# A gather ring on one Trainium2 core: semaphores by section, or by octet of eight tiles

## What is computed

```python
msgs = features[edge_src] * edge_weight[:, None]
agg = jax.ops.segment_sum(msgs, edge_dst, num_segments=N_NODES, indices_are_sorted=True)
return jnp.einsum('ni,oi->no', agg, W) + b
...
H = jax.nn.gelu(xf @ W1 + b1, approximate=False)
probs = jax.nn.softmax((H @ Wg + bg) / TEMP, axis=-1)
assign = jnp.argmax(probs, axis=-1)
for e in range(Wd.shape[0]):
    y = H @ Wd[e] + bd[e]
    out = out + jnp.where((assign == e)[:, None], probs[:, e:e + 1] * y, 0.0)
...
x = x + _L0_gnn_ref(_layernorm(x, axis=-1), src, dst, edge_weight, L0_gnn_W, L0_gnn_b)
x = x + _L0_ffn_ref(_layernorm(x, axis=-1)[None], ...)[0]
```

## Time and profile before

| | us |
|---|---|
| median of three runs | 4119.44 |
| the three runs | 4086.34, 4121.28, 4119.44 |
| the profiled execution | 4089.45 |
| its span, first to last instruction | 4087.7 |
| busy: PE / PE weight load | 2198.2 (54%) / 1562.5 (38%) |
| busy: POOL / DVE / ACT | 1722.3 (42%) / 1026.6 (25%) / 625.3 (15%) |

### The profile page before, as it was taken

How to read it: one execution, slowest core, us unless ns; L and a number is a source line. 1 busy time by engine, 2 the same in 40 slices (tenths; PEclk the granted TensorE clock), 3 DMA queues, 4 the chain that set the end, 5 groups by cost and what they waited for, 6 DMA issues and landing times.

```text
span 4087.7 us, 40360 instructions
## 1 busy us (share of the span) xinstructions
PE 2198.2 (54%) x10966; PEld 1562.5 (38%) x10967; DVE 1026.6 (25%) x3627; ACT 625.3 (15%) x1189; POOL 1722.3 (42%) x1796
## 2 busy tenths in 40 slices
PE   0145645655573674565557455555645746563355
PEld 0024434443442443433435343343433434342344
DVE  7222223223232222322322222232232222222100
ACT  5001111110110111111112111111101111111111
POOL 2644444444435435345343534534444353433300
PEclk9867877877786786777778677777767767776678
DMA  8433343344324334334333433433343242355232
GB/s 334 132 102 104 101 132 105 104 129 137 106 93 143 102 96 138 99 102 137 120 97 108 147 91 106 141 96 105 119 141 110 90 148 93 107 171 190 91 109 82
DMA packets 198291, 496.84 MB, mean 122 GB/s; under 512 B 45096, under 2 KB 114347, under 8 KB 180688
## 3 DMA queue, kind: packets, MB, share of 16 engines
q0 software_dynamic: 88752, 244.13, 19.7%
q1 hardware_dynamic: 109472, 252.06, 18.3%
HBM read 442.89 MB, written 83.68 MB: 129 GB/s over the span
## 4 chain that ended last, share of the span: by engine, by line
PE 41%; issue 17%; another core or an unknown queue 15%; SPq 10%; DVE 6%; DMA 4%; DVEq 3%; ACT 2%; ACTq 0%; POOL 0%; POOLq 0%
PE psH L624 10%; PE psY L638 9%; PE psH L674 9%; SPq L382 7%; PE psH L704 3%; PE psA L649 2%; SPq L298 2%; PE psE L590 2%; DMA xr<-expert_bins 2%; DMA sorted_rows<-work 1%; PE psT L613 1%; DVEq L298 1%; PE psH L664 1%; PE psA L680 1%
## 5 line engine op out<-in xcount | busy, mean ns | idle before, releaser
L438 POOL DMA_INDIRECT big<-xn_table,src_i x1664 | 1598.1, 960 | 1972.5 <-PE psQ L581 1234.6
L590 PE MATMUL psE<-place,parts 128*128 128x80 f32 x832 | 197.8, 415 | 887.3 <-DVE parts L995 877.5
L590 PEld LDWEIGHTS psE<-place,parts 128*128 128x128 f32 x832 | 175.8, 312 | 953.1 <-DVE parts L995 942.4
L624 PE MATMUL psH<-work,w 128*128 128x256 f32 x1856 | 442.9, 399 | 43.3 <-ACT hidT L505 37.8
L638 PE MATMUL psY<-big,hidT 128*128 128x256 f32 x1856 | 418.3, 381 | 0.0
L624 PEld LDWEIGHTS psH<-work,w 128*128 128x128 f32 x1856 | 369.5, 201 | 124.1 <-ACT hidT L505 40.2
L674 PE MATMUL psH<-work,w 128*128 128x512 f32 (+1 forms) x800 | 385.5, 636 | 53.1 <-ACT hidT L524 50.9
L581 PE MATMUL psQ<-big,sel_narrow 128*32 128x256 f32 x3328 | 291.4, 511 | 178.8 <-issue 125.8
L638 PEld LDWEIGHTS psY<-big,hidT 128*128 128x128 f32 x1856 | 348.8, 190 | 45.4
L613 PE MATMUL psT<-ident,xr 128*128 128x128 f32 x232 | 63.0, 427 | 513.0 <-DMA xr<-expert_bins 257.5
L498 ACT ACTIVATE work<-psT 128x512 f32<-128x512 f32 x58 | 34.6, 597 | 1537.0 <-PE psT L613 839.6
(11 more groups left out here) (216 smaller groups left out, 1780.3 us busy)
## 6 DMA issues: line engine op xcount, KB each, us to landing
big<-in_Wd SPq DMA_DIRECT2D x116, 1024.0 KB
big<-xn_table,src_i POOLq DMA_INDIRECT x1664
expert_bins<-sorted_rows SPq DMA_DIRECT2D x375, 65.0 KB
xr<-expert_bins SPq DMA_DIRECT2D x116, 130.0 KB
big<-in_bd SPq DMA_DIRECT2D x116, 128.0 KB
big<-in_x SPq DMA_DIRECT2D x10, 1280.0 KB, 17.4
xn_table<-big SPq DMA_DIRECT2D x10, 1280.0 KB, 13.5
xg<-in_x SPq DMA_DIRECT2D x25, 512.0 KB
```

The source lines that it names most:

```text
L438: nc.gpsimd.indirect_dma_start(out=xring[:, h * STEP_TILES + j, :], out_offset=None, in_=xn_dram[:, :], in_offset=bass.IndirectOffsetOnAxi ...
L590: mm = nc.tensor.matmul(psE[:, at:at + SPAN], parts[:, o, k * P:(k + 1) * P], place[:, o, :], start=True, stop=True)
L624: mm = nc.tensor.matmul(psH[c // 2 % 2][:, c % 2 * C:(c % 2 + 1) * C], w1[:, k, c * P:(c + 1) * P], xT2[half][:, k, :], start=(k == 0), st ...
```

## The change

The three semaphores of the gathers become six, one for each octet of each section. PE waits for an octet's own semaphore ahead of its eight products, and adds 8 to `s_edge_mm` after each octet in place of 16 after the step. In the rare case `wide == 1` it waits for both octets first, as before. POOL's waits, DVE's and all values of the counts per step are as they were. The semaphore's wait moves behind the load of the step's kind.

```diff
-        s_gath = [sem(f"gathered{h}") for h in range(SECTIONS)]
+        s_gath = [[sem(f"gathered{h}_{o}") for o in range(OCTS)] for h in range(SECTIONS)]
...
-                    ).then_inc(s_gath[h], 16)
+                    ).then_inc(s_gath[h][j // OCT], 16)
...
-                pe.wait_ge(s_gath[h], (g + (SECTIONS - h)) * STEP_TILES * 16 // SECTIONS)
                 wide, = load_columns(quads_i[0:1, bass.ds(g, 1), 0:1].rearrange("a b c -> a (b c)"), PE, 1)
                 with pe.If(wide == 0):
                     pe.wait_ge(s_narrow, g + 1)
                     for o in range(OCTS):
+                        pe.wait_ge(s_gath[h][o], (g + (SECTIONS - h)) * OCT * 16 // SECTIONS)
                         for odd in range(2):
                             for j in range(OCT // 2):
                                 t = h * STEP_TILES + o * OCT + 2 * j + odd
                                 mm = nc.tensor.matmul(psQ[j * LANES:(j + 1) * LANES, o * C:(o + 1) * C],
                                                       sel_narrow[:, t, :], xring[:, t, :],
                                                       start=(odd == 0), stop=(odd == 1))
-                    mm.then_inc(s_edge_mm, STEP_TILES)
+                        mm.then_inc(s_edge_mm, OCT)
...
                 with pe.If(wide == 1):
+                    for o in range(OCTS):
+                        pe.wait_ge(s_gath[h][o], (g + (SECTIONS - h)) * OCT * 16 // SECTIONS)
                     for j in range(STEP_TILES):
```

## The result

The changed kernel takes 4462.7 us (median of four runs, 4445.0 to 4472.56), the kernel before beside it 4105.97 us (4086.34 to 4121.28). The ratio is 1.087, 95% interval 1.080 to 1.094: slower by some 357 us. The profiled execution of the changed kernel takes 4470.04 us, its span is 4468.3 us.

The account below looks back on a forecast made before the run. It took PE's completions, held while POOL gathers, as what delays the chain; POOL isn't the bound. 4089.45 + 10 + 204 + 95 = 4398, rounded 4400 us; range 4060 to 4560 us, the forecast's own 4250 to 4560.

Parts of the forecast that it names:

- The completions of PE are held while POOL gathers, and POOL's pause lets them through: In step two of a pair, DVE and POOL learn of PE's products 13 us late, some 3 us after POOL stops.
- The waits by octet: On PE's queue, one more wait and value per step cost 0.2 us, some 10 us in all (0 to 80).
- the second increment: After each octet on PE, one more increment costs 0 to 0.3 us a step; taken as 0.
- POOL let go sooner, step two: Between items A and B, POOL runs two batches without pause, holding PE's completions longer: net 8.5 us a group, 204 us.
- C: Rival, 0.25: POOL stops eight gathers into the next batch for the held second octet; copy 9.2 us later, 4308 us.
- the early stretch: From 168.1 to 253.2, 64 gathers with only two "remote" waits; transposes L613 were seen 21.2 us late.
- The pair beside SP: Between items B and A, SP's copying and loads come later without POOL's pause: 5 us in 19 groups, 95 us.
- rival A: Nothing reaches POOL earlier: its pause stays, only step one's 1.0 us is won; 4075 us, within 1%, chance 0.22.
- The groups with three steps: In five groups item A today loses 14.53 us to a held L624; gain and loss cancel, 0 (-14 to +9 each).
- The markers: Signs: POOL's 53 short "remote" waits mostly gone, L985 and L498 get long ones, L995's step-two wait about as long.
- B, faster: Rival, 0.15: the second step's completion passes during gathers, winning 5.2 us per chain pair; 3975 us, 3% faster.

Follow-up runs that it names:

- e10: Changed kernel with four POOL rules in successive stretches: as changed, whole step, stop every 8 gathers, stop every 4; 3892.52 us against 4065.91 for the kernel before.
- e11: Kernel before with POOL stopping every 4 gathers until its own have landed, throughout; 3537.18 against 4114.92 us, ratio 0.859, on a holding chip.
- e1: Kernel before with the second increment alone (8 after each octet); 3250.62 against 3247.02 us, ratio 1.001, on a chip that doesn't hold.
- e6: Kernel before with the second increment alone, run again; 3246.53 against 3244.78 us, ratio 1.000, on a second chip that doesn't hold.
- e2: Changed kernel with one increment of 16 after the second octet, leaving only the waits by octet; 3246.95 us, ratio 0.9985, on a chip that doesn't hold.
- e5: Changed kernel again, unchanged, beside the kernel before; 4457.05 against 4093.02 us, ratio 1.090, on a chip that holds.
- e4: Kernel before with a POOL stop inside each batch until its first eight gathers have landed; 3268.33 us, ratio 1.005, on a chip that doesn't hold.
- e9: Kernel before with the odd tiles' products left out, 8 instead of 16 a step; 3213.72 us, ratio 0.990, on a chip that doesn't hold.
- e12: Changed kernel with POOL stopping every 4 gathers in each batch; 3432.91 against 3245.23 us, ratio 1.059, on a chip that doesn't hold.
- e7: Changed kernel with POOL asking for the whole step ahead of tile 0; 3248.41 against 3244.78 us, ratio 1.001, on a chip that doesn't hold.

## Why the prediction was right, and where it wasn't

The forecast was 4400 us, measured 4462.7, inside the range. Against the profiled execution the sum was 4398, and 4470.04 came. The account by its steps:

*The completions of PE are held while POOL gathers, and POOL's pause lets them through.* Right on chips that hold, and shown both ways there: take the pause away and a group costs 13 us more than in the kernel before (e10, first rule), leave it and it costs the same (second), add pauses and it costs 13 and 24 us less (third and fourth), and in e11 the whole kernel is 14% faster. What I had not seen is that this is no property of the kernel: on three other chips nothing is held.

*The waits by octet*, 10 us (0 to 80), and *the second increment*, 0. Neither can be measured: 1.001 and 1.000 in e1 and e6, 0.9985 in e2, and the second rule of e10. The Trainium skill (TensorE: Matmul & The Clock Gate, The cost: per-tile semaphore tail) would have asked for 2.7 us; e1's interval of some 10 us can't tell that from nothing.

*POOL let go sooner, step two.* The step that was partly wrong. I wrote that POOL goes on to the end of two unbroken batches. In 22 of the 23 pairs between A and B it stops at least once, at the first gather of the next batch, at the ninth or at both; in the two shown it goes on at the first (after 0.30 and 1.64 us) and stops at the ninth, for the second octet, as C had it. The forecast gave the second octet's increment no wait: in the first pair shown the first increment is in time by 1111 and the second is held until POOL stops. The one pair that did run unbroken looks as forecast, and takes 89.5 us, 14 more than the 75.5 before. The term was 8.5 us net a group; 11.1 were measured on average, 7.1 in the ten pairs of the first picture (C's price was 6.7) and 14.1 in the twelve with held transposes. The parts of C are right: copy 9.2 us later forecast, 10.4 measured; item B faster by 2.5 forecast. To see the latter: from the first step of A to the first of the pair after B it is 75.11 us before (999.22 to 1074.33) and 83.39 after (1090.01 to 1173.40), so 8.3 us, of which the copy has 10.4, which leaves -2.1. This picture holds in ten of the 23 pairs. In twelve others the rest of the forecast's mechanism comes in after all: L666's transposes are held up to the end of the batch, as the early stretch had shown for L613, and the ten of them with two steps are 161.7 us long on average, 8 us more than the groups near 153.5.

*The pair beside SP*, 5 us in 19 groups. Before and after, the first step after B, and the transposes that wait for SP's load:

```profile
1074.33 1.93 PE L581 MATMUL psQ<-big,sel_narrow 128*32 128x256 f32 x32
...
1118.86 1.11 PE L613 MATMUL psT<-ident,xr 128*128 128x128 f32 x4 [16.03 <-issue]
```

```profile
1173.40 1.93 PE L581 MATMUL psQ<-big,sel_narrow 128*32 128x256 f32 x32
...
1223.29 1.11 PE L615 MATMUL psT<-ident,xr 128*128 128x128 f32 x4 [22.43 <-DMA xr<-expert_bins]
```

44.5 us became 49.9: 5.4 us, almost the number taken, and 6.3 on average of the 18 stretches with two steps. But the reason given isn't it, and that the number fits is luck. The pause stays: in the pair shown POOL starts its batch at 1174.78 and goes on at 1198.20 after 3.23 us of "remote", and in all 22 pairs between B and A with a batch behind them it stops there for 3.1 to 3.8 us. What differs in the pair shown is the start, 1.38 us after the products' in place of 2.24 (1076.57), SP's pieces up to the chain's last load, 3.3 us more, and that load, 4.40 us in place of 1.48; the wait behind it is 0.9 us shorter. Why SP's pieces and the load are slower isn't shown. That these pairs keep their pause, though their first octet was done as early, is rival A's picture, and why they go so and the pairs between A and B don't stays open.

*The groups with three steps*, 0 beside the term between A and B. This was right: the stretch with three steps between B and A takes 87.2 us on average in place of 85.0. Gain and loss cancel as forecast. In the first such stretch DVE's copy of the third step is 11 us later after its products' start (29.8 us in place of 18.8), and ACT's answer to the hidden layer, which was held before, is no longer held. Before:

```profile
685.44 0.69 DVE L995 COPY parts<-psQ 128x512 f32<-128x512 f32 x1 [16.53 <-remote]
708.41 1.57 ACT L505 ACTIVATE hidT<-psH,b 128x256 f32<-128x256 f32 x4 [14.73 <-remote]
```

and after, where L626 (L624 in the kernel before) runs without a break:

```profile
743.32 0.69 DVE L997 COPY parts<-psQ 128x512 f32<-128x512 f32 x1 [27.71 <-remote]
757.68 7.07 PE L626 MATMUL psH<-work,w 128*128 128x256 f32 x32
```

The 8 to 17 us that these groups take longer are for the most part those of their stretch between A and B.

*The sum.* 309 us were forecast, 10 + 204 + 95 + 0; of the 380.6 measured, 255 lie between A and B, 113 in the stretches with two steps between B and A, 11 in those with three. The number was near, but its largest term is an average of two pictures that the forecast didn't have, and its second is right by luck. The markers say so too: L519 (transposes in B) got its long "remote" waits, and L987 has 15 of them, 137.9 us in all and up to 15.7, where L985 had none outside the early stretch; L498 got none. But L995's mean rose to 18.0, neither the forecast's "as long" nor C's 23, and POOL's short waits for "remote" are not gone (60 times, 187.8 us): between B and A they are where they were, and between A and B many moved from a batch's first gather to its ninth.

*The rivals.* A, nothing earlier: its picture is that of the pairs between B and A, but not its price, and it is wrong for the sum. B, faster: no pair shows it. C was the nearest in mechanism for the step and, in ten pairs, in price; its 4308 us fell short by its halved SP term and by the transposes that are held in the other pairs.

## What to carry to other kernels

A wait of an engine that isn't the bound can be what keeps another one going. Before an increment is made earlier, look at what the engine that it frees will do next, and whom its standing still had served; the row for that is the short wait of the idle engine that ends within 0.3 us of a long one elsewhere. Where a profile has many waits without a releaser, run the unchanged kernel on a second chip before explaining them: here that alone was 21% of the time (3245 against 4106 us), more than any change made to the code. And a stop is cheap only within the room that the engine has: here one a batch cost 21 us, and three, which took more than the room, cost 188.

## What the hardware showed that I had not expected

- The same kernel takes 4066 to 4115 us in four of the chip sessions (the one of the result, e5, e10, e11) and 3245 to 3247 us in three (e1 to e4, e6 to e9, e12). Where nothing is held, the mean granted clock of PE is also higher, 0.807 in e7 against 0.754 in the profile before. Why the chips differ wasn't found.
- Where the chip holds, SP's pieces in the chain take 0.70 us late in a batch of gathers. In e7, whose POOL gathers from 1071.77 on, they stay at 0.52:

```profile
1081.63 0.52 SPq L382
1082.40 0.52 SPq L382
1083.18 0.52 SPq L382
```

- A stop of 1.6 us of POOL lets one completion pass and the next is held again (805.94, then 818.46); one of 4.4 us was followed by a stretch in which several passed at once (L590, L666 and L615 between 1126.30 and 1133.17, while POOL gathered on).
- What holds the completions stays open. All that the runs show is that POOL's indirect gathers have to run without a stop, and that the chip is one of some. The Trainium skill (NOTIFIC — the notification-queue block, 7.1 Overflow: three behaviours, one of which stalls the engine) describes a queue that can stall the engine that feeds it; no run here shows whether it has a part in this. Every execution here has the profiler's span beside its time, so no run tells either whether the recording itself has one.
